# A gated cross-attention and mixture-of-experts block on one core: routing six of eight batches ahead of the last one, and copying biases per tile

## What is computed

```python
# attention without a softmax, with a decay mask and rotated, scaled q and k
q, k, v = layernorm(x) @ Wq, ctx @ Wk, ctx @ Wv
q, k = xpos(q), xpos_inverse(k)
x = x + tanh(g_xattn) * ((q @ k.T) * decay_mask) @ v
# mixture of experts: 8 experts, each token goes to its best two
xf = layernorm(x).reshape(2048, 256)
w, idx = top_k(softmax(xf @ Wg.T), 2);  w = w / w.sum(-1)
h1 = xf @ (W1 + B1 A1).T + b1          # hidden 512, per expert, low-rank parts folded
h3 = xf @ (W3 + B3 A3).T + b3
y_e = (silu(h1) * h3) @ (W2 + B2 A2).T + b2
x = x + tanh(g_ffn) * sum over the two experts of w * y_e
```

## Time and profile before

| what | before |
|---|---|
| median of 3 runs | 345.79 us (345.37 to 346.42) |
| the profiled execution: its own time | 345.23 us |
| the profiled execution: its span, first to last instruction | 343.4 us |
| mean granted clock of TensorE | 0.968 |
| busy share of the span: PE, DVE, POOL, ACT | 90%, 76%, 57%, 53% |
| moved by DMA | 43.82 MB |

### The profile page before, as it was taken

The page is one execution under the profiler, slowest core; times in us unless marked ns, Lnnn a source line. Parts: engine busy times, 40 slices in busy tenths (PEclk is TensorE's granted clock), DMA queues, the critical chain, the costliest instruction groups (busy, mean ns, idle before and its releaser), DMA issues.

```text
span 343.4 us, 6837 instructions
## 1 busy us (share of the span) xinstructions
PE 308.8 (90%) x1766; PEld 234.3 (68%) x1766; DVE 259.2 (76%) x638; ACT 183.2 (53%) x387; POOL 194.2 (57%) x171
## 2 busy tenths in 40 slices
PE   8589989999997377999999999999999999999970
PEld 3468777778886324467777777777777777777750
DVE  2679797879996599278877788778877788777850
ACT  4646655666775611265565555655565555655540
POOL 1459886878988616514564556554564556454331
PEclk9899999899999769999999999999999999999997
DMA  7937799899878269403332233333331333234100
GB/s 239 383 79 228 233 295 267 243 269 281 267 224 268 92 154 390 137 12 63 49 51 53 48 63 45 52 61 59 60 46 37 63 60 46 50 57 60 19 0 0
DMA packets 28098, 43.82 MB, mean 128 GB/s; under 512 B 6960, under 2 KB 15536, under 8 KB 27792
## 3 DMA queue, kind: packets, MB, share of 16 engines
q1 hardware_dynamic: 15888, 28.52, 26.5%
q0 software_dynamic: 7488, 9.36, 17.0%
q10 hardware_dynamic: 4688, 5.52, 5.1%
HBM read 31.43 MB, written 10.65 MB: 123 GB/s over the span
## 4 chain that ended last, share of the span: by engine, by line
PE 63%; POOL 9%; DVE 8%; DMA 8%; issue 4%; ACT 4%; SPq 1%; POOLq 1%; ACTq 0%; DVEq 0%
PE bank L497 31%; PE bank L514 15%; POOL WL L700 5%; DMA xs<-x_in 5%; PE bank L505 5%; PE bank L487 2%; PE bank L345 2%; DMA WH<-lora_in 2%; DVE stage L783 2%; ACT WH L578 2%; PE bank L443 1%; PE bank L388 1%; PE bank L450 1%; DVE st L798 1%; PE bank L404 1%
## 5 line engine op out<-in xcount | busy, mean ns | idle before, releaser
L761 POOL DMA_INDIRECT out<-ys,sidx x39 | 61.9, 1586 | 85.6 <-DVE gsel L1010 61.8
L700 POOL TENSOR_TENSOR WL<-stage,WH 128x512 bf16<-128x512 f32 x48 | 60.4, 1279 | 18.1 <-ACT WH L578 17.8
L497 PE MATMUL bank<-WH,xh 128*128 x156 | 56.0, 440 | 0.6 <-ACT xh L658 0.6
L685 ACT ACTIVATE ys<-BB,gsel 128x256 f32 x39 | 19.8, 509 | 55.0 <-DMA out<-ys,sidx 52.9
L497 PE MATMUL bank<-WH,xl 128*128 x156 | 48.9, 394 | 0.0
L751 POOL DMA_INDIRECT xg<-xn_rows,gidx x39 | 38.8, 995 | 15.2 <-issue 12.4
L497 PE MATMUL bank<-WL,xb 128*128 x156 | 47.3, 385 | 0.0
L578 ACT ACTIVATE WH<-stage 128x512 fp32r<-128x512 f32 x48 | 29.6, 631 | 22.4 <-DVE stage L783 22.2
L1025 DVE TENSOR_TENSOR h<-bank,BB 128x512 f32<-128x512 f32 x39 | 27.0, 691 | 15.7 <-PE bank L497 15.6
L664 ACT ACTIVATE gh<-bank 128x512 fp32r<-128x512 f32 x39 | 23.4, 599 | 26.8 <-PE bank L505 26.8
L497 PEld LDWEIGHTS bank<-WH,xl 128*128 128x128 f32 x156 | 29.2, 188 | 7.7 <-DVE xl L1016 0.5
(11 more groups left out here) (132 smaller groups left out, 598.0 us busy)
## 6 DMA issues: line engine op xcount, KB each, us to landing
stage<-w_all_in SPq DMA_DIRECT2D x48, 256.0 KB, 4.1
BB<-biases_in SPq DMA_DIRECT2D x8, 640.0 KB, 9.1
LS<-WH SPq DMA_DIRECT2D x45, 48.0 KB
xs<-x_in SPq DMA_DIRECT2D x8, 256.0 KB, 4.0
cx<-ctxT_in SPq DMA_DIRECT2D x8, 256.0 KB, 4.5
out<-x ACTq DMA_DIRECT2D x8, 256.0 KB, 3.9
xn_rows<-xn ACTq DMA_DIRECT2D x8, 256.0 KB, 5.1
lora_parts<-WH ACTq DMA_DIRECT2D x3, 432.0 KB, 5.2
```

The source lines that it names most:

```text
L497: last = nc.tensor.matmul(dst[:, :], lhs[p][:, c * P:(c + 1) * P], W[:, bass.ds(e * (UNITS * UC) + (2 * kind + c) * UC, HID)], start=(part ...
L700: nc.gpsimd.tensor_tensor(w_dst(WL, s, m), stage[(u * UNITS + m) % NSTAGE][:], w_dst(WH, s, m).bitcast(F32), ALU.subtract).then_inc(s_wl, 1)
L761: nc.gpsimd.indirect_dma_start(out=out_rows, out_offset=bass.IndirectOffsetOnAxis(ap=sidx[:, i:i + 1], axis=0), in_=ys[p][:], in_offset=No ...
```

## The change

**Order.** The pipeline over batches stops after eight steps (s = 0 to 7). What steps 8 and 9 did for batches 6 and 7 is spread over what follows. The first six batches (`JA` = 12 of 16 blocks of 128 tokens) are routed while step 7 runs and after it. A tile of this early part must be full: with `NA` = 16, the first 16 tiles are blocks of 128 pairs which every expert has complete from six batches. Pairs that do not fill a block stay in the expert's virtual columns (`NV` = 64: 24 and `SPARE` = 5 for each expert) and are joined by the pairs of batches 6 and 7 in a second routing, whose VectorE instructions are spread over tiles 0 to 12 (`beside_h1`, `beside_h3`). Tiles 16 to 38 come from it.

**Indices.** Gather and scatter columns are no longer indexed by the tile. For every tile, GpSimd reads a column number from `vid` into a register and copies that column (`one_column`) before each gather and each scatter.

**Memory.** The biases no longer stay in SBUF for all experts. SP reads the tile's expert number into a register and copies 640 KB per tile into a ring of three buffers.

Cut to its core (unchanged bodies that only moved are left out):

```diff
+JA = NJ - 2 * TPB
+JB = NJ - JA
+SPARE = JB + 1
+NV = JA * K + E * SPARE
+NA = NV - E * SPARE - E
+KA, KB, KQ = K * JA, K * JB, 8
+BRING = 3
+SAFE = -(-(JA * P - (E - 1) * (P - 1)) // P)
...
-            for s in range(B + 2):
-                step(s, s % 2, s < B, 1 <= s <= B, s >= 2)
+            for s in range(B):
+                step(s, s % 2, s >= 1, s >= 2)
# SP
-            for e in range(E):
-                sp.dma_start(BB[:, e, :], biases[e:e + 1, :].to_broadcast([P, BCOL])).then_inc(s_bb, 16)
...
+            def load_biases(i):
+                r = i % BRING
+                sp.wait_ge(s_eid, 1 if i < NA else 2)
+                if i == 0:
+                    sp.wait_ge(s_scores, B)
+                elif i == 1:
+                    sp.wait_ge(s_out, B)
+                elif i == 2:
+                    sp.wait_ge(s_x2, B)
+                    sp.wait_ge(s_store, 32 * B)
+                else:
+                    sp.wait_ge(s_h3b, i - BRING + 1)
+                    sp.wait_ge(s_b2g, i - BRING + 1)
+                e = sp.value_load(eid[0:1, i:i + 1], min_val=0, max_val=E - 1)
+                sp.dma_start(BB[r][:], biases[bass.ds(e, 1), :].to_broadcast([P, BCOL])).then_inc(s_bb[r], 16)
# PE, after step 7 (the counts of the first routing run inside it)
+            transposes(xn2, s_xn2Tp)
+            scores(B)
+            logits(B - 2, pL)
+            keep_clock(10, WL, pO)
+            for c in range(KA // KQ):
+                pe.wait_ge(s_hi, c + 1); pe.wait_ge(s_pp, c + 1); pe.wait_ge(s_bs, c + 1)
+                ...  # 16 matmuls into 64 columns
+                if c < KA // KQ - 1:
+                    keep_clock(2, WL, pO)
+            attend(B, v[1])
+            unit(E - 1, 1, 0)
+            unit(E - 1, 1, 1)
+            pe.wait_ge(s_x2, B)
+            keep_clock(12, WL, pO)
# PE, behind tile i: i=0: units 2, 3 of expert 7; 1: units 4, 5 and transposes of batch 7;
#   2: its logits; 4: counts of the second routing; 8: its 16 slot matmuls
# ACT, behind tile i
+                if i == 0:
+                    act.wait_ge(s_nm2, B)
+                    normal(x2, rs2, nm2, xn2, s_xn2)
+                    store_rows(B - 1)
+                    weight_hi(E - 1, 1, 0)
+                    weight_hi(E - 1, 1, 1)
+                if i == 4:
+                    act.wait_ge(s_dl, 2)
+                    nc.scalar.activation(e2B[:], dlB[:], ACT.Exp).then_inc(s_e2, 1)
# POOL
+            def one_column(dst, src, i):
+                v = pool.value_load(vid[0:1, i:i + 1], min_val=0, max_val=NV - 1)
+                nc.gpsimd.tensor_copy(dst[:, i:i + 1], src[:, bass.ds(v, 1)]).then_inc(s_col, 1)
+                column[0] += 1
+                pool.wait_ge(s_col, column[0])
...
+                if i < 3:
+                    weight_lo(E - 1, 1, 2 * i)
+                    weight_lo(E - 1, 1, 2 * i + 1)
# DVE, after step 7
+            pair_gates(1, dlA, e2A, denA, waA, wbA)
+            dve.wait_ge(s_rank, 1)
+            ...  # 12 small instructions from counts to places, as before
+            for c in range(KA // KQ):
+                nc.vector.tensor_tensor(INA[:, r, :], cst..., vlA..., ALU.is_equal)      # 128x512
+                nc.vector.tensor_tensor(BSA[:, c], slots_x, slA..., ALU.is_equal)        # 128x1024, all bf16
+                nc.vector.tensor_tensor(ATA[:, r, :], INA[:, r, :], kjA[:, r, :], ALU.mult)  # 128x512, all bf16
+            ...  # tile numbers, row numbers, row kinds
+            add(E - 2, 0, 4)
+            add(E - 2, 0, 5)
+            masked(B)
+            row_maxima(B - 2, pL); sorted_eight(B - 2); indices(B - 2)
+            residual(B, xs[1])
# DVE, before the bias add of h1 of tile i
+                if i in (0, 1, 2): two adds of expert 7
+                if i == 3: row maxima and top eight of batch 7      4: late_experts
+                if i == 5: late_places   6: late_slots   7: late_rows   8: late_columns (128x1024)
+                if i == 9: late_totals   10: late_values   11: late_shifts   12: late_tiles
# DVE, before the bias add of h3
+                if i == 0: scale and shift of batch 7's norm   3: indices   4: two constants
+                if i == 6: pair_gates(2, ...)    11: row_kinds(2, ...)
             def tile(i, q, first, more):
                 p = q % 2
-                e = dve.value_load(eid[0:1, i:i + 1], min_val=0, max_val=E - 1)
                 if more:
                     gates_of(i + 1, (q + 1) % XBUF)
+                beside_h1(i)
                 pos_wait(dve, s_g, i)
-                biased(h1, pH1, i, e, 0, s_h1, s_h1b)
+                dve.wait_ge(s_bb[i % BRING], 16 * (i // BRING + 1))
+                biased(h1, pH1, i, 0, s_h1, s_h1b)
```

More of the change, by code:

```diff
@@ L152, in flamingo @@
[L152 to L155, removed]
-        tiles = ExitStack()
+        folds = ExitStack()
+        LS = [sb(folds, f"LS{i}", [P, LCOL], F32R) for i in range(2)]
+        stage = [sb(folds, f"stage{i}", [P, UC]) for i in range(NSTAGE)]
+        folds.close()
@@ L165, in flamingo @@
         ys = [sb(tiles, f"ys{p}", [P, D]) for p in range(2)]
[L166 to L167 removed]
+        BB = [sb(tiles, f"BB{r}", [P, BCOL]) for r in range(BRING)]
         tiles.close()
@@ L380, in units @@
                             unit(s - 1, 1 - u, m)
[L382 to L390, removed]
+                pe.wait_ge(s_ctx[u], 16 * (half(s, u) + 1))
+                pos_wait(pe, s_krot, s)
+                for m in range(2):
+                    for c in range(CH):
+                        last = nc.tensor.matmul(pK[:, m * S:(m + 1) * S], wq[:, 1, c, m * P:(m + 1) * P], cx[u][:, c, :],
+                                                start=(c == 0), stop=(c == CH - 1))
+                last.then_inc(s_kproj, 1)
                 if three:
@@ L475, in _ @@
-            keep_clock(22, WL)
+                    pe.wait_ge(s_qrot, s)
+                    logits(s - 2, pL)
+                if two:
+                    attend(s, v[1 - u])
+                else:
+                    pe.wait_ge(s_vtab, 2 * 16)
+                if three:
+                    pe.wait_ge(s_xn2T, s - 1)
+                pe.wait_ge(s_xn, s + 1)
+                transposes(xn, s_xnTp)
+                units(2, 3)
+                if not two:
+                    pe.wait_ge(s_tab, 4 * 16)
@@ new lines, in step, with ranks @@
+                last.then_inc(s_vproj, 1)
+                if s == B - 1:
+                    ranks(1, pK, trimA, onesA, HA, HSA)
+                units(4, 5)
+            def ranks(n, dst, tri, ones, H, HS):
+                pe.wait_ge(s_krot, B)
+                pe.wait_ge(s_H, n)
+                nc.tensor.matmul(dst[:, 0:P], tri, H, start=True, stop=False)
+                nc.tensor.matmul(dst[:, 0:P], ones, HS, start=False, stop=True).then_inc(s_rank, 1)
+            batch_steps(step)
+            pe.wait_ge(s_xn2, B - 1)
@@ L834, in _, with row_maxima, sorted_eight @@
             early_sums = [0]
-            def step(s, u, one, two, three):
+            def row_maxima(b, src):
+                dve.wait_ge(s_logit, b + 1)
+                nc.vector.tensor_copy(L8[:], src[:, 0:TPB * E].rearrange("p (t e) -> p t e", t=TPB)).then_inc(s_L, 1)
+            def sorted_eight(b):
+                dve.wait_ge(s_L, b + 1)
+                pos_wait(dve, s_two, 2 * b)
+                for t in range(TPB):
+                    last = nc.vector.max(M8[:, t, :], L8[:, t, :])
+                last.then_inc(s_top, 1)
@@ new lines, in indices, with masked @@
+            def indices(b):
+                dve.wait_ge(s_top, 2 * b + 1)
+                for t in range(TPB):
+                    last = nc.vector.max_index(I8[:, t, :], M8[:, t, :], L8[:, t, :])
+                last.then_inc(s_top, 1)
+            def masked(s):
+                dve.wait_ge(s_scores, s)
+                pos_wait(dve, s_out, s - 1)
+                nc.vector.tensor_tensor(ret[:, 0:2 * P], pS[:, 0:2 * P], msk[:], ALU.mult)
+                nc.vector.tensor_tensor(ret[:, 2 * P:3 * P], pS[:, 2 * P:3 * P], msk[:, 0:P], ALU.mult).then_inc(s_ret, 1)
@@ L837, in step @@
+            def step(s, u, two, three):
                 b = s - 2
                 weight = lambda m: add(s - 1, 1 - u, m)
[L840 to L849 removed]
@@ L915, in step @@
                     early_sums[0] = sums(xs[1 - u], st1)
-                if one and two:
-                    weight(4)
-                    weight(5)
+                    if two:
+                        weight(4)
+                        weight(5)
+                if s == B - 2:
+                    fixed()
             batch_steps(step)
```

827 lines of the change are left out of this document (507 added, 320 removed).

## The result

The changed kernel takes 389.95 us in the median (388.74 to 391.2), the kernel before 346.11 beside it: ratio 1.127, 95% interval [1.123, 1.131]. I had forecast slower, 356.5, with a range up to 364. The sign was right, the size was far off. The profiled execution has a span of 388.0 us. Some executions of a kernel take over 1.5% longer than its fastest: the medians in this document count them, the ratios and their intervals do not.

What follows compares the result with a forecast made beforehand. TensorE was taken to set the pace at 4.83 us a tile, the scatter chain close behind at 4.60. Span 127.5 + 201.05 + 4.5 + 20.5 + 3.0 - 2.5 = 354.05, plus 2.4: forecast 356.5 us, range 339 to 364.

Steps and rivals of the forecast that it cites:

- The bound and the mechanism: Tile stage: bias copies, on the wire 2.2 us after landing t, make the scatter chain replace TensorE's 4.83 us pace.
- what sharing costs ... I take 0.8: Bias copy beside each scatter: landing 0.8 us later, bounds 0 and 1.6, so the chain needs 5.4 us a tile.
- 20.5 + 3.0 - 2.5: Tiles 3 to 38: 20.5 us for slower pace, 3.0 for heavy tiles exceeding it, 2.5 back from partly empty tiles.
- 2.5 given back by partly empty tiles: Seven tiles are partly empty and were to give back some 2.5 us.
- The first three tiles: Tiles 0 to 2, holding work from steps 8 and 9: cost 4.5 us, range 2 to 6.
- the longest thread: Third bias buffer, filled only after batch 7's rows are stored: tile 2's bias add 14 to 16 us behind first product.
- The start: Preparation before the tiles: first product at 127.5 us, 14.85 us earlier than 142.35.
- the three parts: VectorE's parts of 512 + 1024 + 512 elements before the tiles: 1.8 us each, 5.4 in all, bound above 7.8.
- No cost: Rival: copies cost the scatters nothing that counts, below 0.23 us per landing; 343.1 us, chance 0.34.
- the heavy tiles: Tiles 3 to 12 carrying the second routing: 7.7 us in sum over 4.83 a tile, 3.0 over 5.4.
- GpSimd: Rival: register loads and copied columns before gathers and scatters make GpSimd's round about 5.8 us; 371 us, chance 0.07.
- Turns by fours of rows: Rival: DMA engines alternate between copy and scatter, scatter 0.4 us later, pace 5.0; 346.8 us, chance 0.13.

Runs made afterwards that it cites:

- Without copies: Changed kernel with the 36 bias copies of tiles 3 to 38 left out, those tiles using stale rows: 342.64 us, ratio 0.991.
- With the order mended: ScalarE's tile 2 handles batch 7's rows and two weight units before ys(2): 388.75 us on the changed kernel, 342.47 us on the kernel with shifted copies.
- shifted ones: Changed kernel, each copy for tile i held until tile i-2's second bias add, not i-3's: 345.83 us; with ScalarE's tile 2 also reordered, 342.47 us.
- the run with the columns: Kernel before, with GpSimd's register load and column copy added before every gather and scatter, nothing else: 347.56 us, ratio 1.003.
- The doubled one: Changed kernel with a second 640 KB copy per tile from tile 6 on, into a buffer nobody reads: 444.01 us, ratio 1.279.

## Why the prediction was right in sign and wrong in size

**The bound and the mechanism: right.** The scatters' chain took TensorE's place through copies whose moment is tied to the landings. The times behind it hold: 0.77 us from landing to start (0.64 forecast), and the copies' bytes at t + 2.2, for the landing behind 236.35 is followed by the copy's first row at 238.63. "About 1.0 us of the copy is still to go" holds too.

**The failed step: "what sharing costs ... I take 0.8".** It measured 1.5 to 1.6, my own upper bound. I reasoned that the scatter shares the engines with the 1.0 us of the copy that is left. It does not share: its first row waits until an engine has no row of the copy left, 1.1 us, and its last row waits for the engine that is last with the copy, 1.5. The step put 5.4 us a tile where the trace has 6.35. Terms over the 36 tiles were 20.5 + 3.0 - 2.5 = 21.0; scatters 3 to 35 alone measured 47.7. Without copies the same stretch is 318.69 - 160.44 = 158.25, only 2.9 over before, so copies are 44.8 of the 47.7. The "2.5 given back by partly empty tiles" stands: their seven intervals are 2.6 us shorter in sum than seven of the mean (the scatters with 7 and 10 rows are followed by 5.34 and 5.41 us).

**The first three tiles: too low, 4.5 forecast, 11.6 measured** to scatter 3. Without any later copies it is still 160.44 - 128.38 - 25.24 = 6.8. I had the longest thread right (bias add of tile 2 stood at 143.60, 15.7 us behind the first product, "14 to 16"), but called the rest hidden. Part of what I missed is the order on one queue: I named no work behind `ys(2)`, and TensorE's logits were there. With the order mended the figure falls by 3.0 beside the kernel's own copies (to 8.6) and by 2.6 beside shifted ones (from 9.4 to 160.20 - 128.10 - 25.24 = 6.9). Copies make the rest of the difference down to 6.8. The 2.3 us between 6.8 and my 4.5 stay without a cause.

**The start: right.** The first product came at 127.91, forecast 127.5. The terms were less exact than their sum: VectorE's last rotation ended at 107.2 in place of 105.6, and the residual at 124.3 (123.1); from the idle matmuls to the first product it was 0.8 and not 1.2. The half price for operands that are bf16 throughout holds: 1024 elements took 0.68 us (1.22 in the earlier trace rows, with operands of 32 bits), 512 took 0.42, so the three parts took 4.6 us for my 5.4. The twelve idle matmuls took 2.76 us, inside 2.6 to 4.6:

```profile
111.78 0.68 DVE L1168 TENSOR_TENSOR BSA<-WH 128x1024 bf16<-128x1024 bf16 x1
112.38 0.42 DVE L1171 TENSOR_TENSOR ATA<-INA,WH 128x512 bf16<-128x512 bf16 x1
...
123.56 0.75 DVE L1044 SCALAR_TENSOR_TENSOR x<-bank,tg,xs 128x512 f32<-128x512 f32 x1 [2.34 <-PE bank L479]
...
124.36 2.76 PE L420 MATMUL bank<-WL 128*128 128x512 bf16 x12 [0.34 <-DVE x L1044]
...
127.91 0.73 PE L591 MATMUL bank<-WH,xh 128*128 x2 [0.56 <-ACT xh L804]
```

**The rivals.** "No cost" priced a kernel that I could later run: forecast 343.1, measured 342.64 without the copies and 342.47 with shifted ones. So all terms but the copies' were right within 1 us in sum, and that was luck: the way to scatter 3 lost 6.8 us for a forecast of 4.5, and behind it only 2.9 were lost, where the heavy tiles had most of 7.7. "GpSimd" fell by the run with the columns (347.56, not 371). "Turns by fours of rows" (0.4 us, 346.8) fell by the landings 1.6 us late. The Trainium skill, page "DMA: Bandwidth & Descriptors", section "Queues, rings and completion order", also says that an engine drains a whole packet of typically 9 to 17 descriptors before it turns to another queue. One copy has 128 / 16 = 8 rows on each engine, about one such packet, and that would give the whole 1.6 us of one copy. The single copy agrees (1.6). The doubled one does not: turns by packets would let the scatter in behind the first copy, at 1.6, and it measured 3.1. So I took the smaller of the page's two sizes for a packet, and by neither do the doubled copies come out.

With the measured values in my sum: 354.05 + 0.4 (start) + 7.1 (first tiles, 11.6 - 4.5) + 26.7 (47.7 - 21.0) - 0.2 = 388.05, against a span of 388.0. That it closes says only that no stretch was left out, since the measured terms are differences of the same trace.

**What stays open.** Whether order of arrival is the whole rule: few scatters had a copy due behind them. In the doubled kernel, after 276.79 and 370.43, such a copy's rows mix with the scatter's, and these landings were not earlier (8.04 and 7.14 us). Why a scatter's first row needs 2.2 us from its start, and why the engines end a copy about a microsecond apart, no run here separates. I ran no kernel without the gather; in the tile shown its rows come from 241.54 on, behind most of the scatter's, so it is not what delays the scatter's first row.

## What to carry to other kernels

When a periodic transfer is added to a kernel whose pace is near a chain of small scatters, compare when each one's first bytes reach the DMA engines, not when they are issued. In this kernel a copy that was there first cost its whole wire time per landing. Then choose the moment: an event that the compute engine sets, in place of one that the landing sets, took 44 us of loss away here with one number changed. And on every in-order queue, look at what stands behind the instruction that will wait: here that was TensorE's input, some 3 us.

## Not expected of the hardware

- A copy queued after a scatter overtakes it: issued 1.06 us behind its start, its rows reach the engines first; landings +1.0, +1.6 and +3.1 us for 0.8, 1.6 and 3.2 us of copy.
- Between scatters 3 and 35 of the kernel after, four landings come about a microsecond later still (6.3 to 7.0 us). Behind 243.46 the packets show why: from 247.91 to 248.79 a packet of 16 KB of the kind "instruction" runs, and then the last six rows of the scatter, one after the other on one engine, until 249.42, while the windows show one engine's share busy. Two more of the four have such a packet among the scatter's rows; the fourth, behind 177.05, has slow rows of the copy instead (up to 1.15 us for one, 0.2 in the median).

```profile
248.00:249.00 1.00, 1.00 (x6) 0.44 (x4) 0.05 (x1) 0.00 (x0) 0.00 (x0) 1.00 0.50 131
249.00:250.00 1.00, 0.26 (x2) 0.00 (x0) 0.00 (x0) 0.00 (x0) 0.00 (x0) 1.00 0.07 11
```
